# Sliding attention: one bulk exponent for four of a group's eight heads, with POOL subtracting maxima and DVE summing

## The reference, cut to what matters

```python
q, k, v = split(x @ w_qkv.T)                  # 16 heads of 16
scores = q . k / 4                            # each token sees at most 64 tokens back
scores = where(mask, scores, -inf)
attn = softmax(scores)
x = layernorm(x + (attn . v) @ w_out.T)
```

## Time and profile before

| | us |
|---|---|
| median of 3 runs | 842.44 |
| lowest and highest | 841.97, 847.46 |
| span of the profiled execution | 840.3 |
| busy in it: PE, DVE, ACT, POOL | 702.3, 497.6, 447.6, 215.6 |
| sliding attention's groups, first mask to last reciprocal | 13.3 to 91.6 |

### The profile page before, as it was taken

The page is one execution under the profiler, slowest core; times in us unless marked ns, Lnnn a source line. Parts: engine busy times, 40 slices in busy tenths (PEclk is TensorE's granted clock), DMA queues, the critical chain, the costliest instruction groups (busy, mean ns, idle before and its releaser), DMA issues.

```text
span 840.3 us, 14231 instructions
## 1 busy us (share of the span) xinstructions
PE 702.3 (84%) x4980; PEld 592.1 (70%) x4985; DVE 497.6 (59%) x1102; ACT 447.6 (53%) x1146; POOL 215.6 (26%) x359
## 2 busy tenths in 40 slices
PE   5887879989999998688989999998876259999960
PEld 4565778989899886357778888786765147777750
DVE  2577764685866754885535454454147647677644
ACT  3988574484654744685656454646221046556522
POOL 3455300000100101273223232324003503333324
PEclk9998999999999999899989999999989579999995
DMA  8994002202202200502000000000390111111104
GB/s 314 368 288 118 2 1 79 79 1 80 79 1 83 75 1 12 240 1 76 1 1 1 2 1 1 2 1 2 131 394 26 62 40 45 50 44 44 50 32 150
DMA packets 32259, 62.49 MB, mean 74 GB/s; under 512 B 2724, under 2 KB 26984, under 8 KB 29896
## 3 DMA queue, kind: packets, MB, share of 16 engines
q1 hardware_dynamic: 30184, 56.48, 19.8%
q0 software_dynamic: 2016, 5.22, 1.8%
HBM read 46.24 MB, written 15.55 MB: 74 GB/s over the span
## 4 chain that ended last, share of the span: by engine, by line
PE 52%; DVE 15%; ACT 15%; DMA 7%; issue 5%; POOL 4%; SPq 1%; another core or an unknown queue 0%; POOLq 0%; ACTq 0%; DVEq 0%
PE banks L1664 32%; PE bank L1664 21%; ACT arena L717 4%; DMA ys<-arena 4%; DVE U_split L1157 3%; DMA arena<-xs 2%; ACT U_split L736 2%; ACT arena L955 2%; DVE mx L1111 1%; POOL arena L641 1%; POOL xs L631 1%; POOL rstd L533 1%; ACT arena L755 1%; DVE fh L1333 1%; ACT arena L962 1%
## 5 line engine op out<-in xcount | busy, mean ns | idle before, releaser
L1664 PE MATMUL banks<-U_split 128*128 128x256 f32 (+2 forms) x808 | 172.6, 339 | 5.0 <-DVE U_split L1157 2.9
L1664 PEld LDWEIGHTS banks<-U_split 128*128 128x128 f32 x808 | 121.0, 192 | 23.1 <-issue 7.2
L1664 PE MATMUL bank<-U_split 128*128 128x256 f32 (+1 forms) x864 | 118.2, 294 | 16.1 <-DVE U_split L1157 14.6
L1664 PEld LDWEIGHTS bank<-U_split 128*128 128x128 f32 x864 | 111.2, 199 | 20.4 <-issue 16.5
L736 ACT ACTIVATE U_split<-arena 128x1024 fp32r (+6 forms) x122 | 98.7, 835 | 28.5 <-DVE arena L1583 11.3
L1664 PE MATMUL banks<-arena 128*128 (+4 forms) x632 | 109.1, 379 | 4.9 <-DVE arena L1105 3.9
L1664 PE MATMUL banks<-cst,arena 128*128 128x128 f32 (+1 forms) x594 | 89.2, 282 | 27.0 <-DMA arena<-xs 19.7
L1664 PEld LDWEIGHTS banks<-cst,arena 128*128 128x128 f32 (+1 forms) x594 | 70.5, 144 | 43.0 <-issue 15.5
L955 ACT ACTIVATE arena<-banks,dmx 128x128 f32<-128x128 f32 (+1 forms) x128 | 52.4, 418 | 74.9 <-DVE dmx L1432 74.9
L530 POOL TENSOR_SCALAR rstd<-mv 128x1 f32<-128x1 f32 x48 | 14.0, 291 | 301.9 <-DVE mv L1089 278.8
L1664 PEld LDWEIGHTS banks<-arena 128*128 128x128 f32 (+2 forms) x632 | 77.5, 183 | 17.9 <-DVE arena L1105 5.3
(11 more groups left out here) (217 smaller groups left out, 1229.8 us busy)
## 6 DMA issues: line engine op xcount, KB each, us to landing
arena<-in_w_exp SPq DMA_DIRECT2D x8, 1536.0 KB, 14.4
xs<-arena SPq DMA_DIRECT2D x8, 1032.0 KB, 15.4
arena<-in_ctxT SPq DMA_DIRECT2D x4, 1601.0 KB, 7.6
arena<-in_ctx SPq DMA_DIRECT2D x4, 1536.0 KB
arena<-in_w_f SPq DMA_DIRECT2D x3, 1024.0 KB, 13.2
arena<-xs SPq DMA_DIRECT2D x23, 129.0 KB
w_x<-in_w_x SPq DMA_DIRECT2D x9, 256.0 KB, 8.1
arena<-in_w_oh SPq DMA_DIRECT2D x1, 2048.0 KB, 7.8
```

Source lines behind the costliest of these rows:

```text
L1664: return nc.tensor.matmul(o, w, x, start=start, stop=stop, **k)
```

## The change

Four of a group's eight heads (HS = 4) keep their own exponent with bias and accumulator. For the other four POOL adds the negated maxima to the scores in place (`a_lower`, on the semaphore `a_weights`, which now counts it and the normalisation in turn), ACT takes one exponent over all four (128 x 512), and DVE sums them with a reduction ahead of the reciprocal. The turned weights of all groups but the last are now copied by ACT, one group later than before: `a_weightsT(n - 2)`, between the fourth exponent and the bulk one. On POOL the normalisation of group n-1 now stands in iteration n, ahead of `a_lower(n)`; the two `rstd_of` of a sequence move from i = 0 to i = 1, and the mixed values from ahead of the normalisation at i = 1 to behind `a_lower` at i = 2.

```diff
         def on_act(n):
-            return n % GROUPS in (1, 2)
+            return n < NG - 1
...
+            def a_lower(n):
+                pool.wait_ge(G["a_max"], n + 1)
+                g.tensor_tensor(sm[:, n % 4, HS:H0F, :], sm[:, n % 4, HS:H0F, :],
+                                mx[:, n % 4, HS:H0F].unsqueeze(2).broadcast_to([P, H0F - HS, P]), ALU.add).then_inc(G["a_weights"], 1)
+
+            def a_normalise(n):
+                pool.wait_ge(G["a_rinv"], n + 1)
+                g.tensor_tensor(sm[:, n % 4, :, :], sm[:, n % 4, :, :],
+                                rinv[:, n % 4, :].unsqueeze(2).broadcast_to([P, H0F, P]), ALU.mult).then_inc(G["a_weights"], 1)
             for n in range(NG):
                 b, i = divmod(n, GROUPS)
-                if i == 1:
-                    a_mixed_values(b)
-                if i == 0 and b > 1:
+                if i == 1 and b > 1:
                     for t in range(TPB):
                         rstd_of(2 * (b - 2) + t)
                 if n == NG - 1:
                     for t in range(TPB):
                         rstd_of(2 * (B - 2) + t)
-                pool.wait_ge(G["a_rinv"], n + 1)
-                g.tensor_tensor(...).then_inc(G["a_norm"], 1)
+                if n > 0:
+                    a_normalise(n - 1)
+                a_lower(n)
+                if i == 2:
+                    a_mixed_values(b)
+            a_normalise(NG - 1)
...
                 act.wait_ge(G["a_max"], n + 1)
-                for h in range(H0F):
+                for h in range(HS):
                     a.activation(sm[:, n % 4, h, :], sm[:, n % 4, h, :], ACT.Exp, bias=mx[:, n % 4, h:h + 1],
                                  accum_out=rsum[:, n % 4, h:h + 1]).then_inc(G["a_exp"], 1)
-                if n >= 1 and on_act(n - 1):
-                    a_weightsT(n - 1)
+                if n >= 2:
+                    a_weightsT(n - 2)
+                act.wait_ge(G["a_weights"], 2 * n + 1)
+                a.activation(sm[:, n % 4, HS:H0F, :], sm[:, n % 4, HS:H0F, :], ACT.Exp).then_inc(G["a_exp"], 1)
...
+            a_weightsT(NG - 2)
...
             def a_rinv(n):
-                dve.wait_ge(G["a_exp"], H0F * (n + 1))
+                dve.wait_ge(G["a_exp"], (HS + 1) * (n + 1))
+                link(v.tensor_reduce(rsum[:, n % 4, HS:H0F], sm[:, n % 4, HS:H0F, :], AX, ALU.add))
                 v.reciprocal(rinv[:, n % 4, :], rsum[:, n % 4, :]).then_inc(G["a_rinv"], 1)
...
                 a_max(n)
-                if n >= 2 and not on_act(n - 2):
-                    a_weightsT(n - 2)
...
             def a_transpose(n):
-                pe.wait_ge(G["a_norm"], n + 1)
+                pe.wait_ge(G["a_weights"], 2 * n + 2)
```

More of the change, by code:

```diff
@@ L51 @@
 H0F = H0 // KT
+HS = H0F // 2
 CTX = 1601
@@ L351, in build @@
             const_set ln_var ln_rstd ln_done xT_raw xT_done
-            a_q a_k a_v a_q_sb a_k_sb a_v_sb a_vmix a_s a_add a_max a_exp a_rinv a_norm
+            a_q a_k a_v a_q_sb a_k_sb a_v_sb a_vmix a_s a_add a_max a_exp a_rinv a_weights
             a_pt a_pt_act a_pt_dve a_o a_o_sb a_y a_y_sb ld_rest
@@ L544, in a_mixed_values @@
                 real = lambda w, lo, hi: vpad[lo:hi, b % 2, w, :].rearrange("p (h c d) -> p h c d", c=4, d=D0)[:, :, 0:4:3, :]
-                pool.wait_ge(G["a_norm"], GROUPS * b + 1)
+                pool.wait_ge(G["a_weights"], 2 * GROUPS * b + 2)
                 for j, (w, lo, hi) in enumerate(((1, 0, WIN), (0, WIN, P))):
@@ L559, in _ @@
                         rstd_of(2 * (B - 2) + t)
-                pool.wait_ge(G["a_rinv"], n + 1)
-                g.tensor_tensor(sm[:, n % 4, :, :], sm[:, n % 4, :, :],
-                                rinv[:, n % 4, :].unsqueeze(2).broadcast_to([P, H0F, P]), ALU.mult).then_inc(G["a_norm"], 1)
+                if n > 0:
[4 more added lines that the diff above has]
+            a_normalise(NG - 1)
             pool.wait_ge(G["ld_zero_exp"], 16 * (NE + 1))
```

## The result

| | before | after |
|---|---|---|
| median (runs of the first comparison) | 843.08 us (4) | 854.68 us (4), 850.02 to 861.12 |
| ratio, 95% interval | | 1.0142 [1.0103, 1.018] |
| ratio in a second comparison, 6 and 23 runs | | 1.0120 [1.0085, 1.0155] |
| first mask to r(15) | 78.09 us | 89.81 us |
| r(15) to the first scores of cross-attention | 7.26 | 7.26 |

855.0 was forecast and 854.68 measured: slower by 11.6 us by the medians. The groups' stage grew by 11.72 us, against 11.6 in the sum.

The account below looks back on a forecast made before the run. The prediction took a loop of waits between ACT and DVE, no full engine, as the bound. Steps added 11.6 us and half-clock projections 1.0, taking the span from 840.3 to 852.9; with 2.1 for the median, 855.0, range 849.5 to 862.

Parts of the forecast that it names:

- r(15): Start of DVE's reciprocal of group 15, the last of sliding attention: forecast at 102.98 us against 91.36, +11.6 us.
- The steady step: Time between reciprocals of successive steady groups, set by the ACT-DVE loop: 5.11 us against 4.55 before.
- POOL under cover: POOL's loop of normalisation and a_lower: 4.64 us, under 5.11, so hidden in steady groups, binding in group 1.
- Group 8: Long step where ln_end waits for rstd, now behind a_lower: 7.28 us against 5.52 before.
- Group 12: Long step like group 8's, with ln_end waiting for rstd behind a_lower: 7.28 us.
- Group 15: Last step, with two rstd now ahead of normalisation 14 and a_lower(15): 8.91 us against 5.72 before.
- The projections at half clock: PE's projections around the last reciprocal, slowed after near idleness: 0 to 3.0 us possible, 1.0 taken.
- this follows r(15) as before: DVE's parts and cross-attention's first scores keep their distance from the last reciprocal: 7.26 us.
- A: Rival: a_lower costs as much as the normalisation (1.9), so POOL's loop, 5.54, binds: 863 us; chance 0.07.
- B: Rival: PE's clock halves for several groups, projections cost the full 3.0: +4, 859 us; chance 0.15.
- C: Rival: the shift is taken up later, or terms are at their low ends: 851 us; 0.13 for 842 to 851.
- D: Rival: ACT's total work sets the pace, -9.8 us, giving 832.6 us; chance 0.04.

Follow-up runs that it names:

- b2: Kernel before, with DVE's sum over four heads also done ahead of the reciprocal, its result unread: 850.3 us, ratio 1.0113 to the kernel before.
- a1: Changed kernel, with ACT's copy of turned weights behind the bulk exponent instead of ahead of it: 850.7 us, ratio 1.0107 to the kernel before.
- a4: Changed kernel, with POOL's subtraction a_lower done twice, first into an unread spare tile: 863.2 us, ratio 1.0282 to the kernel before.
- a2: Changed kernel, with rstd back ahead of the normalisation at i = 0 and the last pair behind a_lower(15): 847.1 us, ratio 1.0062 to the kernel before.
- b5: Kernel before, with only the two rstd of a sequence moved early, to i = 3: 840.9 us, ratio 0.9982 to the kernel before.
- a3: Changed kernel with both the copy behind the bulk exponent and rstd moved early: 844.1 us, ratio 1.0046 to the kernel before.
- c1: Changed kernel reordered: DVE's maximum before sum and reciprocal, POOL's a_lower before rstd and normalisation, ACT's copy behind the bulk exponent: 840.6 us, ratio 0.9989 to the kernel before.
- b1: Kernel before with one swap on DVE, max(n) ahead of the reciprocal of group n-1: 836.1 us, ratio 0.9933 to the kernel before.

## Why the prediction was right, step by step

- **The steady step.** 5.11 worked out, 5.15 measured. The 0.04 are DVE's sum, 0.685 and not 0.64: it costs as much out of SBUF as out of PSUM, so the upper of the two rows was the right one. b2 shows the sum's term whole (0.71 on each step). a1 shows 0.55 of the copy's 0.91, as POOL's loop takes over there; the rest of that term is read from the chain.
- **POOL under cover.** 4.64 worked out, 4.60 measured in group 1. a4 shows the distance.
- **Group 8**: 7.28 and 7.23. **Group 12**: 7.28 and 7.07; its first rstd followed a_lower sooner. **Group 15**: 8.91 and 8.82. a2 removes all three. For the kernel before, the prediction put step 12 down to rstd as it did step 8; the chain and b5 show a second cause as long, PE's late transposes and ACT's copies behind them. The sum doesn't use it.
- **r(15)**: + 11.6 worked out; + 11.7 measured from the first mask. Its absolute place was 0.4 earlier than forecast, as the first mask came 0.5 earlier (12.73 us, before 13.27).
- **The projections at half clock**: the mechanism was there (the sixteen matmuls of the earlier trace rows took 4.55 in place of 3.62, and the transposes ahead of them 1.97), the price was mis-sized: 1.0 taken, 0 measured, as the lag stayed at 7.26. The cover was used up to the last: PE ended 7.28 us after r(15), against 5.8 at full clock by the prediction and 7.26 for DVE's way. So "this follows r(15) as before" held in the number and not in the path, which now goes through PE; that the two ways came out equal is luck. a1, a2, a3 and c1 have lags 1.4 to 3.9 longer: there the projections started later against r(15) as well (1.6 to 3.0 us behind it), and the cover was gone.
- **The total** thus came out right with one term of 1.0 too many; the measured difference moves by more than that between comparisons (12 us at ratio 1.0142, 10 at 1.0120), and single runs by 11 us (850.0 to 861.1). That forecast and median are 0.3 us apart is luck; the stage's 11.7 us against 11.6 isn't.
- **Rivals.** A stayed 0.55 us away (a4). B took place in part: the granted clock was 0.50 from 80 to 83 us and 0.63 from 86 to 89, in groups 12 and 13, under cover, and 0.50 again from 98 to 101. C fell: bulk exponent, sum and a_lower came at 0.62, 0.685 and 1.04, not at their low ends. D, ACT's total as the bound, fell: ACT's busy time went from 447.6 to 439.4 us and the kernel got slower. But its condition, max(n) ahead of r(n-1), proved to be the one that pays in the stage (b1).

The Trainium skill's page "ScalarE: Activation LUTs" (What ACT_TABLE_LOAD costs) gives 0.71 us for the bulk exponent with a pointer bias, an estimate worked out from its figures. L736 took 0.618, so that price isn't the one paid here.

## What to carry to other kernels

Draw the loop before counting busy time: an operation moved from a fuller engine to an emptier one costs its whole length if it lands on the loop, and the one that left may have been beside it. In an in-order program the place of a small operation (a 0.9 us copy between two exponents, a pair of rstd behind one more instruction) can cost more than the operation. The first thing to try in such a loop is to take an operation that needs nothing from the previous round out of the previous round's wait: one swap of two lines gained 0.7% here (2.9 us or 0.3% of it in the stage that it touches), where a rebuilt softmax lost 1.4%. And the place where a time is won or lost should be looked up before it is put down to a change: profiles of one and the same program behind the stage differed by up to 15 us.

## What the runs showed of the hardware

- The granted clock after a wait of PE differs between executions of the same instructions: after 3.1 us of waiting, the same eight matmuls took 2.02 in one execution and 3.61 in another, which moved a whole step by 1.6 us.
- DVE's scaling of 128x256 by two per-row operands (ln_end) took 0.41 us, and 1.12 to 1.99 when it began while POOL's tensor_tensor of 128x1024 ran, until just behind that one's end. DVE's maximum of 128x1024 wasn't held so: it took 1.17 us with POOL's normalisation running beside it.
- POOL's fp32 addition of 128x512 with a broadcast operand took 1.04 us and the multiplication of 128x1024 took 1.90: an estimate from the two, if both operations go at one rate, is 1.68 ns for each further element and 0.18 us for the instruction.
- DVE's reduction of 512 fp32 took 0.685 us from SBUF into four sums; from PSUM into one it had taken 0.686.
